# Graph-attention kernel: the queue and the place from which twelve adjacency loads are issued

## The chip, the cores and the metric

The kernel runs on one core of one Trainium2 chip. The metric is the device time of one execution in microseconds, the median over several executions.

## What is computed

The layer is a graph attention with 16 heads over 2048 nodes, followed by a residual and a layer norm. The adjacency matrix is 2048 x 2048 in f32, and x is 2048 x 512.

```
seq = (x @ W_seq).reshape(N, H, DH)              # N 2048, H 16, DH 32
scores = leaky_relu(score1[:, :, None] + score2[:, None, :], 0.2)
scores = scores + (1.0 - adj)[None] * -65500.0
hidden = einsum('hij,jhd->ihd', softmax(scores), seq).reshape(N, 512)
out = layernorm(x + elu(hidden @ W_out + b_out))
```

## The kernel before

The 2048 nodes are 16 tiles of 128 rows. All tiles, loops and loads are counted from 0 here, so the first adjacency tile is 0 and the last is 15.

**First stage (to about 51 us).** For each tile t of x, SyncE loads it (`load_x`, L298, 256 KB), TensorE turns it (`turn_x`, L387), ScalarE copies the turned tile out of PSUM (`copy_x`, L581), and TensorE multiplies it with the first half of the weights (`project`, L400). TensorE's order is: turn tile t+1, project tile t, turn tile t+2, project tile t+1. Turning tile t needs its load; projecting it needs its copy. VectorE copies the results (`copy_first`, L787 and L788).

**The adjacency.** Beside this the adjacency matrix goes through four steps, tile by tile:
1. a load of 1 MB of f32 into one of `STAGE` = 4 buffers (`load_adj`, L303). Tile t uses the buffer t % 4, so from tile 4 on it waits until the cast of tile t - 4 is done (semaphore `adj_cast`);
2. a cast to int8 by ScalarE (`cast_adj`, L592), which also sums the row;
3. a correction of empty rows by VectorE (`fix_adj`, L779 and L782);
4. a DMA transpose from `tring` to `adj8`, issued by SyncE (`turn_adj`, L316).

ScalarE's order is written out by hand. While x is projected, iteration t copies tile t+1 and then casts the tiles that the table `CAST_AT` (L57) gives for it: tile 0 at t = 1, tile 1 at t = 2, tile 2 at t = 4, tile 3 at 6, tile 4 at 7, tile 5 at 9, tile 6 at 11, tile 7 at 13 and tile 8 at 14. Copies of the first head's row (`copy_row0`, L601) lie between them. Casts 9 to 15 are in the second stage (L656 to L682), between copies of the second projection (`copy_second`, L597), two exponentials (L663, L665), and the high halves of the values (`split_high`, L631), for each of which VectorE makes the input (`values`, L860) and then the low half (`split_low`, L866).

SyncE's order is written out too. It issues x tiles 0 to 7 and adjacency tiles 0 to 3 alternately (L310 to L326), and then the loop over t below: the load of adjacency tile t + 4, two x tiles, the transpose of tile t. Each instruction of SyncE waits for those ahead of it, so the load of tile t + 5 comes behind the transpose of tile t. An x load from tile 6 on waits until TensorE has turned the tile six before.

```
            for t in range(NT):
                if t + STAGE < NT:
                    load_adj(t + STAGE)
                for n in range(8 + 2 * t, min(10 + 2 * t, NT)):
                    load_x(n)
                turn_adj(t)
```

**Second stage (about 51 to 93 us).** TensorE makes the second half of the projection (`project_second`, L416) and the first products of head 0 (L475); ScalarE and VectorE make the values of the first heads and the masks of head 0 (ScalarE: L614; VectorE: L811, joined with the adjacency in L816). Masks go into the slots of `tring` that the transposes have read.

**Third stage (from about 93 us).** For each head, TensorE multiplies masks with values (L475), with the sums over the plain adjacency behind (L489). The output projection and the layer norm follow (L556, L568 and further).

Of the kernel before, what the change touches and what calls it, by code (L numbers as in the profile page):

```python
# [16 lines left out]
NT = N // P  # L17
# [25 lines left out]
XS, STAGE, TURNED = 6, 4, 8  # L43
# [50 lines left out]
def gat_kernel(nc, x, adj, W_seq, a1, a2, W_out, b_out, out):  # L94
    with ExitStack() as ctx:
# [3 lines left out]
        def sem(name):  # L99
            return ctx.enter_context(nc.semaphore(name))  # L100
# [25 lines left out]
        stage = flat[:, 4 * HV:4 * HV + 2 * STAGE * N].bitcast(F32).rearrange("p (r n) -> p r n", r=STAGE)  # L126
# [56 lines left out]
        adj_loaded = [sem(f"adj_loaded{r}") for r in range(STAGE)]  # L183
# [4 lines left out]
        adj_cast, noedge_set, adj_fixed = (sem(s) for s in ("adj_cast", "noedge_set", "adj_fixed"))  # L188
# [31 lines left out]
        adj_n = adj.rearrange("(q p s) n -> q s p n", p=P, s=2)  # L220

        def x_t(t):
            return x_n[t // 2, t % 2]
# [12 lines left out]
        def wait_turned(eng, it):  # L236

            eng.wait_ge(adj_turned[it % TURNED], 16 * (it // TURNED + 1))
# [34 lines left out]
        def row(h):  # L273

            return abc[:, (h + 1) % 2, :] if h > 0 else row0
# [8 lines left out]
        def load_a(eng, r, a):  # L284

            eng.dma_start(a_row[:, r, :].rearrange("p (q d) -> p q d", d=DH),
                          a.rearrange("(o q d) -> o q d", o=1, q=1).to_broadcast([1, P // DH, DH])).then_inc(a12_loaded, 16)

        def load_w(eng, k):
            eng.dma_start(Wx[:, k, :, 0:half], W_seq[k * P:(k + 1) * P, :].rearrange("p (s c) -> p s c", s=2)).then_inc(w_loaded[k], 16)  # L290


        @block.sync
        def _(sp):
            def load_x(t):
                if t >= XS:
                    sp.wait_ge(x_turned, t - XS + 1)
                sp.dma_start(xs[:, t % XS, :], x_t(t)).then_inc(x_loaded[t % XS], 16)  # L298

            def load_adj(t):  # L300
                if t >= STAGE:
                    sp.wait_ge(adj_cast, t - STAGE + 1)
                sp.dma_start(stage[:, t % STAGE, :], adj_n[t // 2, t % 2]).then_inc(adj_loaded[t % STAGE], 16)  # L303

            load_a(sp, 0, a1)
            load_x(0)
            for k in range(0, KT, 2):
                load_w(sp, k)
            for t in range(1, XS - 2):
                load_x(t)  # L310
            def turn_adj(it):

                sp.wait_ge(adj_fixed, it + 1)
                if it >= TURNED:
                    wait_turned(sp, it - TURNED)
                sp.dma_start(adj8[:].bitcast(F16)[:, :, it * P:(it + 1) * P],  # L316
                             tring[:, it, :].bitcast(F16), transpose=True).then_inc(adj_turned[it % TURNED], 16)

            load_adj(0)
            load_x(4)  # L320
            load_adj(1)
            load_x(5)
            load_adj(2)
            load_x(6)
            load_adj(3)
            load_x(7)  # L326
            for t in range(NT):
                if t + STAGE < NT:
                    load_adj(t + STAGE)
                for n in range(8 + 2 * t, min(10 + 2 * t, NT)):  # L330
                    load_x(n)
                turn_adj(t)

            sp.wait_ge(a_copied, 1)
            for t in range(4):

                sp.dma_start(scratch.rearrange("h (g t n) -> t h g n", g=4, t=4)[t],
                             aT[2 * H * t:2 * H * t + H, :].rearrange("p (g n) -> p g n", g=4)).then_inc(a_stored[t], 16)
            for t in range(4):
                sp.wait_ge(a_stored[t], 16)  # L340
            for h in range(1, H):
                if h == 2:
                    sp.wait_ge(seq2_made, NT)
                if h >= 2:
                    sp.wait_ge(t_ready, NT * (h - 1))
                if h == 5:

                    sp.wait_ge(mx2_ready, 1)
                    sp.dma_start(scratch2.rearrange("o (p h) -> (o p) h", p=P), mx2).then_inc(mx2_stored, 16)
                    sp.wait_ge(mx2_stored, 16)  # L350
                    sp.dma_start(peaks, scratch2[0:1, :].partition_broadcast(P)).then_inc(peaks_loaded, 16)
                sp.dma_start(row(h), scratch[h:h + 1, :].partition_broadcast(P)).then_inc(abc_loaded[h % 2], 16)

            sp.wait_ge(t_ready, NT * (H - 1))
            sp.dma_start(Wo_sb, W_out.rearrange("(k p) n -> p k n", p=P)).then_inc(wo_loaded, 16)
            sp.wait_ge(t_free, NT * (H - 2))
            sp.dma_start(bout, b_out.rearrange("(o d) -> o d", o=1).partition_broadcast(P)).then_inc(bout_loaded, 16)
            for i in range(NT + 2):
                r = i % 2
                if i < NT:  # L360
                    if i >= 2:
                        sp.wait_ge(y_ready, i - 1)
                    sp.dma_start(xr[:, r, :], x_t(i)).then_inc(xr_loaded[r], 16)
                if i >= 2:
                    if i <= NT:
                        sp.wait_ge(out_ready, i - 1)
                    else:
                        sp.wait_ge(out_last, 1)
                    sp.dma_start(out_n[(i - 2) // 2, i % 2], ot[:, r, :]).then_inc(stored[r], 16)
            for q in range(2):  # L370
                sp.wait_ge(stored[q], 16 * NT // 2)
# [202 lines left out]
        def _(act):  # L574
            load_a(act, 1, a2)
            for k in range(1, KT, 2):
                load_w(act, k)
# [9 lines left out]
            def cast_adj(it):  # L587
                r = it % 4
                act.wait_ge(adj_loaded[it % STAGE], 16 * (it // STAGE + 1))
                if it >= 4:  # L590
                    act.wait_ge(noedge_set, it - 3)
                act.activation(tring[:, it, :], stage[:, it % STAGE, :], ACT.Copy, scale=EDGE,  # L592
                               accum_out=deg[:, r:r + 1]).then_inc(adj_cast, 1)

            def copy_second(t):
                act.wait_ge(seq2_made, t + 1)
                act.copy(seq[:, t, HALF:H, 0:DH], second_bank(t).rearrange("p (h d) -> p h d", d=DH)).then_inc(seq2_copied, 1)  # L597
# [18 lines left out]
            for t in range(NT):  # L616
                if 0 < t < NT - 1:
                    copy_x(t + 1)
                for it in CAST_AT.get(t, ()):
                    cast_adj(it)  # L620
                if t in (5, 9, 13):
                    copy_row0(t // 4 - 1)
# [31 lines left out]


            cast_adj(9)  # L656
            copy_second(0)
            copy_row0(3)
            cast_adj(10)
            copy_second(1)  # L660
            copy_second(2)
# [74 lines left out]
            for i in range(NT):  # L736
                r, q = i % 2, (i - 1) % 2
                if i >= 2:
                    act.wait_ge(y_ready, i - 1)
                for n, (c, _) in enumerate(column_parts(i, r)):  # L740
                    act.wait_ge(z_ready, i + 1 + n)

                    act.activation(et[:, r, c], zt[:, r, c], ACT.Relu, scale=-1.0).then_inc(zneg_ready, 1)  # L743
                    act.wait_ge(zneg_ready, i + 1 + n)
                    act.activation(et[:, r, c], et[:, r, c], ACT.Exp, scale=-1.0).then_inc(e_ready, 1)
                if i + 2 < NT:
                    turn_hidden(i + 2)
                if i >= 1:
                    act.wait_ge(shift_ready, i)
                    if i >= 3:  # L750
                        act.wait_ge(stored[q], 16 * ((i - 1) // 2))
                    act.activation(ot[:, q, :], yt[:, q, :], ACT.Identity, bias=shift[:, q:q + 1],  # L752
                                   scale=rstd[:, q:q + 1]).then_inc(out_ready, 1)
# [419 lines left out]
```

## Time and profile before

| what | value |
|---|---|
| median of 3 runs | 519.34 us (519.14 to 520.39) |
| profiled execution, its own time | 520.75 us |
| its span | 519.0 us |
| TensorE matmul busy | 501.0 us (97%) |
| VectorE busy | 460.2 us (89%) |
| ScalarE busy | 433.0 us (83%) |
| DMA queue of SyncE (q1) | 51.79 MB, 30.2% of 16 engines' span |
| DMA queue of ScalarE (q10) | 0.52 MB, 0.3% |
| adjacency loads, issue to landing | 16, median 8.4 us |

Busy shares are of the span, from the profiler; 1.75 us of the profiled execution lie outside its span. The granted TensorE clock is at its full level in all of the 40 slices but the last. A DMA has two times in the profile: the issue, which keeps the issuing engine's queue, and the landing, when the data is there and the semaphore rises. Busy shares of the DMA engines are sums of the packets' times, and can be over 1 where packets overlap.

### The profile page before, as it was taken

What the parts mean: (1) busy time and instruction counts of PE and PEld (TensorE: products, weight loads), DVE (VectorE), ACT (ScalarE), POOL (GpSimd) and SP (SyncE); (2) the same over time, 40 slices, a digit from 0 to 9 for tenths busy, and PEclk for the clock granted to TensorE, in tenths of its full rate; (3) what the DMA queues carried; (4) which work ended last, traced back from release to release, by engine and by line L of the source; (5) the groups of instructions that cost most, each with busy time, mean ns of one, the idle gap of its engine ahead of it and who ended that gap; (6) DMA issues with size and microseconds to landing.
All of it is one profiled execution on the core that took longest, in us unless ns stands there. A gap on an engine that the chain in (4) does not pass through costs nothing.

```text
span 519.0 us, 15251 instructions
## 1 busy us (share of the span) xinstructions
PE 501.0 (97%) x6744; PEld 454.4 (88%) x6744; DVE 460.2 (89%) x577; ACT 433.0 (83%) x462; POOL 34.8 (7%) x64
## 2 busy tenths in 40 slices
PE   8999999999999989999999999999999999899993
PEld 7888888999999989999999999999999999644542
DVE  3457679998999999999999999999998879988886
ACT  2776779798999889999999999999995989266664
POOL 3000000000000010000000000000000000035444
PEclk9999999999999999999999999999999999999998
DMA  7999993402020301202021020202202040025443
GB/s 249 414 313 343 342 304 72 164 3 82 3 83 2 124 30 55 83 3 83 3 83 56 30 83 3 83 1 83 80 7 82 3 144 3 1 68 155 125 142 120
DMA packets 30721, 53.28 MB, mean 103 GB/s; under 512 B 18496, under 2 KB 19776, under 8 KB 26688
## 3 DMA queue, kind: packets, MB, share of 16 engines
q1 hardware_dynamic: 30104, 51.79, 30.2%
q8 instruction: 53, 0.87, 0.7%
q10 hardware_dynamic: 552, 0.52, 0.3%
q14 instruction: 12, 0.10, 0.1%
HBM read 43.78 MB, written 4.33 MB: 93 GB/s over the span
## 4 chain that ended last, share of the span: by engine, by line
PE 73%; DVE 13%; ACT 6%; issue 4%; DMA 3%; POOL 0%; ACTq 0%; DVEq 0%; POOLq 0%; SPq 0%
PE sums L475 35%; PE bank L489 18%; PE sums L568 10%; PE sums L400 6%; DVE tring L816 4%; ACT tring L614 3%; DVE tring L811 3%; DMA Vp<-in_adj_dram 1%; PE bank L556 1%; PE sums L387 1%; DVE Vp L866 1%; DMA Vp<-in_L_gnn_W_seq_dram 1%; DVE Vp L792 1%; ACT Vp L631 1%; DVE xp L860 1%
## 5 line engine op out<-in xcount | busy, mean ns | idle before, releaser
L614 ACT ACTIVATE tring<-abc,ab 128x2048 int8<-128x2048 f32 x150 | 292.4, 2023 | 2.7 <-DMA abc<-a_rows 2.7
L475 PE MATMUL sums<-Vp,tring 128*128 128x132 f16 x4096 | 241.6, 221 | 3.6 <-DVE tring L816 1.9
L475 PEld LDWEIGHTS sums<-Vp,tring 128*128 128x128 fp8e4 x4096 | 236.9, 98 | 5.6 <-issue 3.5
L816 DVE TENSOR_TENSOR tring<-adj,tring 128x1024 uint32<-128x1024 uint32 (+1 forms) x134 | 155.9, 1174 | 11.7 <-ACT tring L614 7.5
L489 PE MATMUL bank<-Vp,adj 128*128 128x132 f16 x2048 | 126.1, 221 | 3.3 <-DVE Vp L866 3.3
L489 PEld LDWEIGHTS bank<-Vp,adj 128*128 128x128 fp8e4 x2048 | 122.1, 96 | 3.7 <-DVE Vp L866 3.6
L811 DVE TENSOR_SCALAR tring<-abc,ab 128x2048 int8<-128x2048 f32 x90 | 115.5, 1284 | 0.0
L568 PE MATMUL sums<-abc,Vp 128*128 128x512 f32 (+1 forms) x136 | 57.5, 568 | 0.1
L568 PEld LDWEIGHTS sums<-abc,Vp 128*128 128x128 f32 x136 | 24.7, 190 | 22.7 <-issue 22.0
L652 ACT ACTIVATE low<-sums 128x33 f32<-128x33 f32 (+3 forms) x66 | 20.1, 393 | 22.3 <-PE sums L475 22.3
L592 ACT ACTIVATE tring<-Vp 128x2048 int8<-128x2048 f32 x16 | 30.6, 1914 | 5.9 <-DMA Vp<-in_adj_dram 5.9
L752 ACT ACTIVATE Vp<-Vp 128x512 f32<-128x512 f32 x15 | 12.2, 813 | 16.4 <-POOL Vp L1146 16.4
L866 DVE SCALAR_TENSOR_TENSOR Vp<-Vp,xp 128x528 f16<-128x528 f16 x32 | 21.2, 706 | 3.6 <-ACT Vp L631 3.6
L879 DVE TENSOR_TENSOR cab<-low,sums 128x66 f32<-128x66 f32 (+3 forms) x33 | 21.2, 682 | 1.4 <-ACT low L652 1.4
L637 ACT ACTIVATE acc<-bank 128x132 f32<-128x132 f32 x64 | 18.8, 294 | 2.8 <-PE bank L489 2.7
L631 ACT ACTIVATE Vp<-xp 128x528 f16<-128x528 f32 x32 | 19.6, 678 | 1.7 <-DVE xp L860 1.7
L860 DVE TENSOR_TENSOR xp<-acc,Es 128x1056 f32<-128x1056 f32 x16 | 20.1, 1254 | 0.1
L811 DVE TENSOR_SCALAR tring<-cab,ab 128x2048 int8<-128x2048 f32 (+2 forms) x16 | 14.7, 950 | 3.1 <-DMA adj<-tring 2.5
L743 ACT ACTIVATE Vp<-Vp 128x512 f32<-128x512 f32 (+1 forms) x17 | 10.2, 602 | 8.3 <-DVE Vp L1042 8.2
L1042 DVE TENSOR_TENSOR Vp<-sums,Vp 128x512 f32<-128x512 f32 (+1 forms) x17 | 11.2, 658 | 6.6 <-PE sums L568 6.6
L400 PE MATMUL sums<-Vp,acc 128*128 128x288 f32 x64 | 17.0, 406 | 0.0
L787 DVE COPY ab<-sums 128x32 f32<-128x32 f32 x16 | 3.0, 189 | 13.7 <-PE sums L400 13.7
(116 smaller groups left out, 370.3 us busy)
## 6 DMA issues: line engine op xcount, KB each, us to landing
Vp<-in_adj_dram SPq DMA_DIRECT2D x16, 1024.0 KB, 8.4
abc<-a_rows SPq DMA_DIRECT2D x15, 1024.0 KB, 4.8
abc<-in_x_dram SPq DMA_DIRECT2D x16, 256.0 KB, 7.3
Vp<-in_x_dram SPq DMA_DIRECT2D x16, 256.0 KB, 3.0
out_dram<-Vp SPq DMA_DIRECT2D x16, 256.0 KB, 2.2
abc<-in_L_gnn_W_out_dram SPq DMA_DIRECT2D x1, 1024.0 KB, 5.3
Vp<-in_L_gnn_W_seq_dram ACTq DMA_DIRECT2D x2, 256.0 KB, 5.4
Vp<-in_L_gnn_W_seq_dram SPq DMA_DIRECT2D x2, 256.0 KB, 6.1
```

What stands on the lines that cost most here:

```text
L400: mm = pe.matmul(first_bank(t), xT_part(t, k), Wx[:, k, 0, :], start=(k == BY_VECTOR[0]), stop=(k == BY_VECTOR[1]))
L475: mm = pe.matmul(bank[b][:, c * 2 * VW:(c + 1) * 2 * VW], slot(jt)[:, it * P:(it + 1) * P].bitcast(F8), Vp[:, h, jt, :, :], start=(jt == 0 ...
L489: mm = pe.matmul(bank[6 + s % 2][:, 0:GRP * HW], edge_bytes[:, jt // 2, it * P:(it + 1) * P, jt % 2].bitcast(F8), Vp[:, GRP * g:GRP * (g + ...
L568: mm = pe.matmul(into, hT[:, q, k * P:(k + 1) * P], Wo_sb[:, k, c], start=(k == 0), stop=(k == KT - 1))
L592: act.activation(tring[:, it, :], stage[:, it % STAGE, :], ACT.Copy, scale=EDGE, accum_out=deg[:, r:r + 1]).then_inc(adj_cast, 1)
L614: return act.activation(slot(jt)[:, columns], row(h)[:, columns], ACT.Sign, bias=ab[:, jt, H + h:H + h + 1], scale=-1.0)
L631: high = act.activation(Vp[:, k, :, 0, s * HW:(s + 1) * HW], xp[:, :, s, :], ACT.Copy, scale=1.0 / LO[s])
L811: return dve.tensor_scalar(slot(jt)[:, columns], row(h)[:, columns], ab[:, jt, H + h:H + h + 1], -1.0, ALU.is_gt, ALU.mult)
L816: return dve.tensor_tensor(words, edges, words, ALU.bitwise_and)
L860: dve.tensor_tensor(xp[:], seq[:, :, k, :].unsqueeze(2).to_broadcast([P, NT, 2, HW]), Es[:, :, :, k:k + 1].to_broadcast([P, NT, 2, HW]), A ...
L866: low = dve.scalar_tensor_tensor(out=Vp[:, k, :, 1, s * HW:(s + 1) * HW], in0=Vp[:, k, :, 0, s * HW:(s + 1) * HW], scalar=-LO[s], in1=xp[: ...
L879: return dve.tensor_tensor(into, lo, high, ALU.add)
```

## The change

`load_adj` becomes a helper that takes the issuing engine. SyncE keeps the loads of adjacency tiles 0 to 3. The loads of tiles 4 to 15 leave SyncE's loop, and ScalarE issues each one directly behind the cast of the tile four before; ScalarE waits for that cast (`adj_cast`) ahead of the issue. Buffers, semaphores, casts and transposes are unchanged.

```diff
+        def load_adj(eng, t):
+            if t >= STAGE:
+                eng.wait_ge(adj_cast, t - STAGE + 1)
+            eng.dma_start(stage[:, t % STAGE, :], adj_n[t // 2, t % 2]).then_inc(adj_loaded[t % STAGE], 16)
...
-            def load_adj(t):
-                if t >= STAGE:
-                    sp.wait_ge(adj_cast, t - STAGE + 1)
-                sp.dma_start(stage[:, t % STAGE, :], adj_n[t // 2, t % 2]).then_inc(adj_loaded[t % STAGE], 16)
...
-            load_adj(0)
+            load_adj(sp, 0)
...
             for t in range(NT):
-                if t + STAGE < NT:
-                    load_adj(t + STAGE)
                 for n in range(8 + 2 * t, min(10 + 2 * t, NT)):
                     load_x(n)
                 turn_adj(t)
...
                 act.activation(tring[:, it, :], stage[:, it % STAGE, :], ACT.Copy, scale=EDGE,
                                accum_out=deg[:, r:r + 1]).then_inc(adj_cast, 1)
+                if it + STAGE < NT:
+                    load_adj(act, it + STAGE)
```

## Rows read from the trace of the kernel before

**Rows 1.** The chain that ended last, in order of time (start us, us, what).
```profile
56.62 7.50 DMA Vp<-in_adj_dram
...
67.34 1.34 DVE Vp L866 x2
...
93.11 9.38 PE sums L475 x160
```

**Rows 2.** Busy time by stretches: from:to and length, engines (instructions), PEclk, DMA share, GB/s.
```profile
10.00:25.00 15.00, 15.00 (x91) 12.55 (x90) 8.30 (x20) 9.28 (x14) 1.07 (x1) 1.00 1.02 419
...
10.00:51.40 41.40, 41.40 (x224) 33.89 (x223) 24.22 (x63) 27.47 (x39) 1.07 (x1) 1.00 1.07 361
...
68.00:93.00 25.00, 23.17 (x224) 21.01 (x222) 24.55 (x34) 21.64 (x29) 0.00 (x0) 1.00 0.61 179
```

**Rows 3.** Waits: ScalarE from 51 to 68 us, then all from 0 to 70 us (total, times, longest).
```profile
ACT tring L592 <- DMA Vp<-in_adj_dram: 4.6, 4, 2.8
...
DVE Vp L866 <- ACT Vp L631: 3.6, 1, 3.6
```

**Rows 4.** SyncE in order of time (start us, us, instruction).
```profile
17.81 0.33 SPq L303 DMA_DIRECT2D Vp<-in_adj_dram  x1
...
19.14 6.82 SPq L316 DMA_TRANSPOSE adj<-tring  x1
26.01 0.57 SPq L303 DMA_DIRECT2D Vp<-in_adj_dram  x1
```

**Rows 5.** Line 298, stretches 1.6 to 1.8, 8.5 to 13 and 13 to 13.6 us.
```profile
L298 SPq DMA_DIRECT2D abc<-in_x_dram x1: 479/479/479, 1.6 to 1.6; - x1
...
DMA to landing us min/median/max: 2.7/2.7/2.7
...
L298 SPq DMA_DIRECT2D abc<-in_x_dram x1: 666/666/666, 8.8 to 8.8; - x1
...
DMA to landing us min/median/max: 13.5/13.5/13.5
...
L298 SPq DMA_DIRECT2D abc<-in_x_dram x1: 328/328/328, 13.4 to 13.4; - x1
...
DMA to landing us min/median/max: 12.1/12.1/12.1
```

**Rows 6.** Line 303, stretch 8.1 to 9 us.
```profile
L303 SPq DMA_DIRECT2D Vp<-in_adj_dram x1: 592/592/592, 8.2 to 8.2; - x1
...
DMA to landing us min/median/max: 13.6/13.6/13.6
```

**Rows 7.** TensorE in order of time, 17 to 35 us.
```profile
22.23 2.11 PE L400 MATMUL sums<-Vp,acc 128*128 128x288 f32 x8
...
24.61 0.60 PE L387 MATMUL sums<-Vp,abc 128*128 128x128 f32 x4
...
26.99 0.60 PE L387 MATMUL sums<-Vp,abc 128*128 128x128 f32 x4
```

**Rows 8.** ScalarE in order of time.
```profile
2.06 1.28 ACTq L290 DMA_DIRECT2D Vp<-in_L_gnn_W_seq_dram  x2
...
17.59 0.19 ACT L592 ACTIVATION_READ_ACCUMULATOR tring<-Vp 128x1 f32 x1
...
18.16 1.91 ACT L592 ACTIVATE tring<-Vp 128x2048 int8<-128x2048 f32 x1
...
22.92 1.91 ACT L592 ACTIVATE tring<-Vp 128x2048 int8<-128x2048 f32 x1
...
48.49 1.93 ACT L592 ACTIVATE tring<-Vp 128x2048 int8<-128x2048 f32 x1
...
66.05 1.19 ACT L631 ACTIVATE Vp<-xp 128x528 f16<-128x528 f32 x2
```

**Rows 9.** DMA queues, 4.5 to 6.5 us (packets, MB, share of 16 engines).
```profile
q1 hardware_dynamic: 252, 0.25, 40.8%
q10 hardware_dynamic: 265, 0.25, 36.6%
```

More of the change, by code:

```diff
@@ L317, in turn_adj @@
                              tring[:, it, :].bitcast(F16), transpose=True).then_inc(adj_turned[it % TURNED], 16)
-            load_adj(0)
+            load_adj(sp, 0)
             load_x(4)
-            load_adj(1)
+            load_adj(sp, 1)
             load_x(5)
-            load_adj(2)
+            load_adj(sp, 2)
             load_x(6)
-            load_adj(3)
+            load_adj(sp, 3)
             load_x(7)
             for t in range(NT):
-                if t + STAGE < NT:
-                    load_adj(t + STAGE)
                 for n in range(8 + 2 * t, min(10 + 2 * t, NT)):
```

## The prediction

> **What bounds the kernel now.** I read the chain that ended last first, because it names the stretch in which the change acts. It runs through TensorE up to 51 us, then through a load of an adjacency tile (56.62 to 64.1 us), the low half of head 0's values on VectorE at 67.34, and back into TensorE at 93.11 [rows 1]. The busy times say why. From 10 to 51.4 us TensorE is busy for all of 41.40 us: any hole there moves the end. From 68 to 93 us VectorE is busy for 24.55 of 25 us, so what counts between 51 and 67 us is when its run from 67.34 can begin [rows 2]. That run waits 3.6 us for ScalarE's `split_high` [rows 3], which stands behind casts 9 to 12, and these four wait 4.6 us for their loads [rows 3]. This wait is what the change can win.
>
> The third view is the DMA share: 1.02 from 10 to 25 us at 419 GB/s, and 1.07 up to 51.4 us [rows 2]. The DMA engines have no idle time in the first stage. Whatever is brought forward there pushes something else back.
>
> **What SyncE's queue does.** Tile 4's load is issued at 17.81. Two x loads and transpose 0 follow, whose issue holds SyncE for 6.82 us from 19.14, and only then, at 26.01, comes the load of tile 5 [rows 4], though cast 1 ran from 18.16 to 20.07 [rows 8]. So the loads of 5 and later are some 5 us late against their casts, as the diff has it. They are also behind all x loads issued before them, in one queue.
>
> **The change part by part.**
>
> *Twelve issues leave SyncE.* One takes 0.33 to 0.59 us in the rows read [rows 4, 6], so about 7 us go. SyncE is not on the chain. The x loads and transposes behind them are issued earlier; I cost that at nothing, the cover being the full DMA queue.
>
> *Twelve issues come to ScalarE.* Its own two weight loads took 1.28 us, 0.64 each [rows 8]. Before each, ScalarE now waits until the cast has ended with its row sum, at 17.78 for cast 0 [rows 8]; I put 0.1 us on that wait. I take 0.64 + 0.1 = 0.75 us each. In the first stage, the copy of an x tile is what queues behind the issue, and TensorE wants it 2.4 us after the turn (22.23 to 24.61 is one period [rows 7]); the copy takes 0.6 us. So 1.8 us of lateness is covered, and one issue fits. Two casts in consecutive iterations make 1.5 us: it fits too. If the issue took 1 us or more, 0.2 us or more per such pair would show. Cost here: 0.
>
> *Between 48.49 and 66.05* ScalarE goes from cast 8 to `split_high` of head 0 [rows 8]. Four loads (tiles 12 to 15) are now issued within it, behind casts 8 to 11: 4 x 0.75 = 3.0 us. Cast 8 itself starts 0.8 us late behind the load issued after cast 7. The waits of casts 9 to 12 for loads vanish, since these are now issued 8 us and more before use: 4.6 us [rows 3]. Sum: 3.0 + 0.8 - 4.6 = -0.8 us; VectorE's run would begin 0.8 us earlier, and all behind it with it. The bounds: with issues of 0.33 us, 4 x 0.43 + 0.4 - 4.6 = -2.5 us; with 1.3 us each, twice the rows', 5.6 + 1.4 - 4.6 = +2.4 us.
>
> *The order on the DMA engines.* The load of tile 4 used to stand behind x tiles 6 and 7 in SyncE's queue. It now has a queue of its own. How two queues share the engines is seen where the weights are loaded from both: between 4.5 and 6.5 us q1 moved 252 packets and q10 265 [rows 9]: packet by packet, one each. An adjacency packet is a row of 8 KB, an x packet one of 2 KB. At 419 GB/s a tile of 1 MB takes 2.5 us and an x tile 0.6 us [rows 2]. Both have 128 packets, so beside an adjacency load an x tile takes 0.6 + 2.5 = 3.1 us, and another adjacency tile 5.0 us.
>
> [...]
>
> Now the walk. Before, tile 2 landed at 8.2 + 13.6 = 21.8 [rows 6], x6 at 8.8 + 13.5 = 22.3 and x7 at 13.4 + 12.1 = 25.5 [rows 5]. TensorE wanted x6 at 24.61 and x7 at 26.99 [rows 7]: 2.3 and 1.5 us to spare. An x load alone lands after 2.7 us [rows 5], of which 0.6 is data, so an issue acts on landings some 2.1 us later.
> 1. Tile 4, issued by ScalarE behind cast 0 at 17.85, acts from 19.9. By then tile 2 has 1.9 us to go, 6 packets of 8 per engine. Alternating, it takes 3.8 us: tile 2 lands at 23.7.
> 2. Cast 1, 0.8 us later than before, ends at 20.9, so tile 5 is issued at 21.0 and is there. x6 alternates with it: 3.1 us, landing at 26.8. TensorE is 2.2 us late.
> 3. Cast 2 runs at 23.8 instead of 22.92 [rows 8], so tile 6 is issued at 25.8 and acts from 27.9. Tile 3 has 8 packets: 2 beside the end of tile 5 (1.25 us, 28.0), 6 beside tile 6 (3.75 us, 31.8).
> 4. x7 has two packets of tile 6 beside it: 1.2 us, landing at 33.0. TensorE wanted it at 26.99: 6.0 us late in all (x6's 2.2 us are within it).
>
> Then it ends, because copy 7 stands ahead of cast 3 on ScalarE, and so no load of tile 7 is issued until x7 is there. x8 and x9 have the engines nearly to themselves, and later x loads find ScalarE's loads 2.4 us and more apart. The bounds: if only tile 4 gets ahead of x7, 25.5 + 2.5 = 28.0, a stall of 1.0 us; if tiles 4 and 5 do, 3.5 us. I take 6.0, since the weights' packets alternated one to one. Below 1.0 us it needs a queue of ScalarE that yields.
>
> The 6.0 us are not won back. ScalarE's copies and casts 3 to 8 follow TensorE, and from cast 8 to `split_high` ScalarE would run without waits, so `split_high` comes 6.0 - 0.8 = 5.2 us later; VectorE's full run and head 0 with it. TensorE has 1.8 us of idle time between 68 and 93 us [rows 2], which does not help, since VectorE is the one that is full.
>
> **Sum.** 6.0 - 0.8 = +5.2 us: the profiled execution of 520.75 (span 519.0) would take 526.0. It stands 1.4 us above the median of the runs shown; I put the difference on the median: 519.3 + 5.2 = 524.5 us. A measurement of this kernel can tell about 0.3%, 1.6 us, from no change.
>
> **Rivals.**
>
> *The issue on ScalarE waits for SyncE's transposes.* Tile 5's load would be issued at 21.0, in the middle of transpose 0's 6.82 us, which end at 25.96 [rows 4]. If one issue excludes the other, ScalarE stands 4.9 us, the copy of x4 ends at 27.2 instead of before 22.23 [rows 7], and TensorE loses about 4.9 us. Tiles 5 and 6 then come too late to hurt x7. The issues behind casts 9 to 11 would meet transposes too, which between 51 and 67 us hold SyncE most of the time. Of their lengths only transpose 0's is in my rows; as an estimate I take a fifth to a quarter of its 6.8 us for each of the three, 4 us. Sum: 4.9 + 4 - 0.8 = +8.1, 527.4 us. Against it: in the rows, ScalarE's two issues beside SyncE's took only 0.64 us each [rows 8], but no transpose was there. [...] No row of before shows it or excludes it. Chance 0.23.
>
> *A milder jam.* Tile 4, or tiles 4 and 5, get ahead of x7: stalls of 1.0 to 3.5 us, in all +0.2 to +2.7, so 519.5 to 522.0 us. Chance 0.15, a fifth of it within 0.3%.
>
> *Not slower: x keeps its place.* If ScalarE's queue delays x6 by less than 2.3 us and x7 by less than 1.5 us, TensorE sees nothing and only ScalarE's sum counts: -0.8, 518.5 us. The deciding point is whether x7 still lands before 26.99. Against it stand the DMA share of 1.02 and one packet each in the weights. Chance 0.15.
>
> *Faster by more:* the same with issues of 0.33 us, -2.5, so 516.8 us. Chance 0.05.
>
> **How the numbers follow.** The forecast has 0.42: 524.5 us. Slower by over 0.3% (above 520.9) holds forecast, first rival and four fifths of the milder jam: 0.42 + 0.23 + 0.12 = 0.77. Within 0.3%: 0.15 + 0.03 = 0.18. Faster: 0.05. The range leaves out the fastest case and, above, a lock that costs more than I put on it: from 518.5, the case without a jam, to 528.5, the first rival with 1 us more. The forecast's own range, with stalls of 4 to 7 us, is 522.5 to 525.5.
>
> **What would show it.** In the profile after: TensorE, busy throughout from 10 to 51 us before, has holes in front of L387 between 24 and 34 us, which wait for a DMA of x. The landing of x7 grows from 12.1 to some 19 us. Tile 5's load is issued near 21 us from ScalarE's queue, with 0.6 us; if it takes some 5 us instead, the first rival is right, and the hole lies before L400 near 22 us and waits for ScalarE's copy. The waits of casts 9 to 13 for loads are gone. VectorE's first L866 starts near 72.6 instead of 67.34, and the heads' steady part starts as much later. If TensorE has no hole before 51 us, the forecast is wrong; if it has one and the end does not move, my claim that VectorE's run carries it through is.

## The result and the profile after

The changed kernel takes 554.81 us (median of 4 runs, 550.29 to 567.88); the kernel before took 519.52 us beside it (519.14 to 520.39). The ratio is 1.0639, with a 95% interval of 1.0603 to 1.0674: slower by 35.3 us in the medians. The ratio leaves out the longest of the changed kernel's runs, which stands over 1.5% above the fastest; the median of the other three is 551.84 us, 32.3 us above the kernel before. I had forecast 524.5 us and a range up to 528.5. The direction was right, the size was not: the loss is over six times the 5.2 us that I had worked out, and outside the range.

The profiled execution is the longest of the four, 567.88 us with a span of 566.1 us. A second profile of the same kernel, further down, has a span of 542.5 us and the same pattern, milder. First the page of the longest: busy time, then the span in 40 slices of 14 us.

```profile
PE 513.0 (91%) x6744; PEld 462.8 (82%) x6744; DVE 460.4 (81%) x577; ACT 434.0 (77%) x462; POOL 34.8 (6%) x64
...
PE   9955537698999999899999999999999999999994
...
DVE  3431118199999999989999999999999878988886
ACT  2632344467999998889999999999998699646764
...
PEclk9986787989999999899999999999999999999998
DMA  8999899984220103112021020120220103004443
GB/s 287 416 113 246 190 40 264 161 102 123 76 77 1 77 2 114 34 45 76 2 76 76 2 78 19 59 76 2 76 77 2 76 6 129 1 20 145 135 130 130
```

The busy times of VectorE and ScalarE are those of before within 1 us (460.2 and 433.0 us). What has grown is mostly idle time, in slices 3 to 10; TensorE's busy time has grown too, from 501.0 to 513.0 us, where its granted clock is lower. The DMA share stays at 8 and 9 tenths up to slice 9, where before it was down to 3 tenths in slice 7, but in slices 3 to 6 the GB/s are 113, 246, 190 and 40, where the kernel before moved 304 to 343. The same in stretches (from:to and length, the engines, PEclk, DMA share, GB/s), first the changed kernel:

```profile
10.00:25.00 15.00, 15.00 (x91) 12.52 (x89) 7.08 (x19) 9.00 (x14) 0.00 (x0) 1.00 1.02 417
25.00:50.00 25.00, 12.97 (x54) 9.23 (x53) 5.79 (x16) 6.89 (x10) 0.00 (x0) 0.81 1.09 187
50.00:76.00 26.00, 19.41 (x80) 15.00 (x78) 3.76 (x10) 12.45 (x17) 0.00 (x0) 0.79 1.20 182
76.00:105.00 29.00, 16.98 (x76) 14.07 (x75) 14.34 (x38) 12.91 (x22) 0.41 (x1) 0.82 1.13 179
```

The kernel before:

```profile
25.00:50.00 25.00, 25.00 (x129) 20.20 (x128) 14.52 (x39) 17.68 (x24) 0.00 (x0) 1.00 1.11 327
50.00:76.00 26.00, 25.26 (x143) 21.45 (x142) 19.48 (x41) 18.70 (x31) 0.40 (x1) 1.00 1.11 338
```

Up to 25 us nothing has changed: 417 GB/s at a share of 1.02, before 419 at 1.02 [rows 2]. From 25 us on the share stays above 1, and the rate falls to 179 to 187 GB/s up to 105 us. Before, it was 327 and 338 GB/s at 1.11 from 25 to 76 us. The DMA engines are reported as full as before, and move little more than half as much. The granted clock of TensorE is at a mean of 0.79 to 0.82 here, a mix of stretches at full level (1.00 from 31.0 to 36.9 us) and at half of it (0.50 from 44 to 54 us); from 25 to 50 us it was busy for only 12.97 us.

The chain that ended last names what is waited for, and [rows 1] is its counterpart (start us, us, what):

```profile
27.40 21.15 DMA abc<-in_x_dram
...
54.75 28.32 DMA adj<-tring
...
94.53 16.88 DMA adj<-tring
...
138.82 9.38 PE sums L473 x160
```

Before, there was one adjacency load of 7.50 us in it. Now there is an x load of 21 us and two transposes of 28 and 17 us. The piece of 160 products, with which the steady part of the heads begins, starts at 138.82 instead of 93.11 us, 45.7 us later, and the span is 47.1 us longer (566.1 against 519.0): little was lost behind it. In the second profile the piece of 160 products begins at 116.65, 23.5 us later, and the span is 23.5 us longer.

The next rows are ScalarE in order of time (start us, us, instruction), to compare with [rows 8]; line 292 is `load_adj` here:

```profile
17.52 0.36 ACTq L292 DMA_DIRECT2D Vp<-in_adj_dram  x1
...
20.44 0.33 ACTq L292 DMA_DIRECT2D Vp<-in_adj_dram  x1
```

SyncE in order of time, to compare with [rows 4]:

```profile
18.45 8.90 SPq L316 DMA_TRANSPOSE adj<-tring  x1
...
30.01 16.16 SPq L316 DMA_TRANSPOSE adj<-tring  x1
...
54.75 76.46 SPq L316 DMA_TRANSPOSE adj<-tring  x13
```

ScalarE's issues take 0.33 to 0.36 us, also the one at 20.44, in the middle of transpose 0's 8.90 us. SyncE is held for 16.16 us by transpose 1, and the last 13 transposes keep it for 76.46 us. The view of line 316, all transposes (count: ns min/median/max, first and last start), and then the landings of the same 16 in the kernel before:

```profile
L316 SPq DMA_TRANSPOSE adj<-tring x16: 1232/4670/16157, 18.4 to 130.0; - x16
...
DMA to landing us min/median/max: 3.1/17.4/28.3
```

```profile
DMA to landing us min/median/max: 3.1/7.8/11.0
```

The view of line 303, `load_x` here, once around 13.1 us (x7) and once around 27.4 us (x10), to compare with [rows 5]:

```profile
L303 SPq DMA_DIRECT2D abc<-in_x_dram x1: 328/328/328, 13.1 to 13.1; - x1
...
DMA to landing us min/median/max: 13.7/13.7/13.7
...
L303 SPq DMA_DIRECT2D abc<-in_x_dram x1: 1792/1792/1792, 27.4 to 27.4; - x1
...
DMA to landing us min/median/max: 21.1/21.1/21.1
```

Before, the 16 transposes landed after 3.1 to 11.0 us, 7.8 in the median. Now the median is 17.4 us and the longest takes 28.3; in the second profile the median is 9.1 us and the longest 26.3, so there it is a few transposes that are very slow. x7 took 1.6 us more than before [rows 5] and landed at 26.8, but x10 took 21.1 us. TensorE in order of time shows what that did, with [rows 7] for before (in brackets the idle time ahead and what ended it):

```profile
26.89 0.66 PE L385 MATMUL sums<-Vp,abc 128*128 128x128 f32 x4
...
29.89 0.66 PE L385 MATMUL sums<-Vp,abc 128*128 128x128 f32 x4 [0.40 <-DMA abc<-in_x_dram]
...
35.54 0.66 PE L385 MATMUL sums<-Vp,abc 128*128 128x128 f32 x4 [3.05 <-DMA abc<-in_x_dram]
36.03 3.15 PE L398 MATMUL sums<-Vp,low 128*128 128x288 f32 x8
...
48.59 1.11 PE L385 MATMUL sums<-Vp,abc 128*128 128x128 f32 x4 [8.55 <-DMA abc<-in_x_dram]
```

The hole that I had forecast at x7 is not there. The holes begin with x8 (0.40 us), and the large one, 8.55 us, is x10's. The row at 36.03 also shows the lower clock: eight products take 3.15 us at a granted clock of 0.64 in the mean, and 2.11 us at the full one [rows 7].

### The profile page after: what moved, and what is told of

Read it like the earlier page. It is cut to its first block, busy times and chain, and to the rows that moved or that the text cites. A ratio compares the mean times of both kernels' runs of the same rounds, so it can differ in the third digit from the quotient of the medians.

```text
span 566.1 us, 15251 instructions
## 1 busy us (share of the span) xinstructions
PE 513.0 (91%) x6744; PEld 462.8 (82%) x6744; DVE 460.4 (81%) x577; ACT 434.0 (77%) x462; POOL 34.8 (6%) x64
## 2 busy tenths in 40 slices
DMA packets 30721, 53.28 MB, mean 94 GB/s; under 512 B 18496, under 2 KB 19776, under 8 KB 26688
## 4 chain that ended last, share of the span: by engine, by line
PE 66%; DVE 13%; DMA 12%; ACT 5%; issue 4%; POOL 0%; DVEq 0%; POOLq 0%; ACTq 0%
PE sums L473 32%; PE bank L487 17%; PE sums L566 9%; DMA adj<-tring 8%; DMA abc<-in_x_dram 4%; DVE tring L816 4%; DVE tring L811 3%; ACT tring L614 3%; PE sums L398 3%; PE bank L554 1%; DVE Vp L866 1%; PE sums L385 1%; PE sums L377 1%; DVE Vp L792 1%; PE sums L414 1%
## 5 line engine op out<-in xcount | busy, mean ns | idle before, releaser
L487 PE MATMUL bank<-Vp,adj 128*128 128x132 f16 x2048 | 127.7, 222 | 3.4 <-DVE Vp L866 3.4
L487 PEld LDWEIGHTS bank<-Vp,adj 128*128 128x128 fp8e4 x2048 | 123.8, 97 | 3.8 <-DVE Vp L866 3.8
L652 ACT ACTIVATE low<-sums 128x33 f32<-128x33 f32 (+3 forms) x66 | 20.1, 393 | 23.9 <-PE sums L473 23.9
L385 PE MATMUL sums<-Vp,abc 128*128 128x128 f32 x64 | 11.6, 312 | 18.6 <-DMA abc<-in_x_dram 18.6
L385 PEld LDWEIGHTS sums<-Vp,abc 128*128 128x128 f32 x64 | 8.9, 160 | 22.3 <-DMA abc<-in_x_dram 20.9
L414 PE MATMUL sums<-Vp,acc 128*128 128x256 f32 x64 | 16.1, 409 | 12.0 <-DVE acc L788 12.0
L752 ACT ACTIVATE Vp<-Vp 128x512 f32<-128x512 f32 x15 | 12.2, 813 | 16.4 <-POOL Vp L1146 16.4
L414 PEld LDWEIGHTS sums<-Vp,acc 128*128 128x128 f32 x64 | 12.9, 208 | 14.4 <-DVE acc L788 12.5
L866 DVE SCALAR_TENSOR_TENSOR Vp<-Vp,xp 128x528 f16<-128x528 f16 x32 | 21.2, 706 | 0.0
## 6 DMA issues: line engine op xcount, KB each, us to landing
Vp<-in_adj_dram ACTq DMA_DIRECT2D x12, 1024.0 KB, 18.6
```

The lines of the kernel that those rows point to most:

```text
L385: mm = pe.transpose(bank[r][:, k * P:(k + 1) * P], xs[:, t % XS, k * P:(k + 1) * P], idf)
L414: mm = pe.matmul(second_bank(t), xT_part(t, k), Wx[:, k, 1, 0:half], start=(k == 0), stop=(k == KT - 1))
L487: mm = pe.matmul(bank[6 + s % 2][:, 0:GRP * HW], edge_bytes[:, jt // 2, it * P:(it + 1) * P, jt % 2].bitcast(F8), Vp[:, GRP * g:GRP * (g + ...
L652: copied = act.activation(into, made, ACT.Copy, scale=1.0 / LO[s])
L866: low = dve.scalar_tensor_tensor(out=Vp[:, k, :, 1, s * HW:(s + 1) * HW], in0=Vp[:, k, :, 0, s * HW:(s + 1) * HW], scalar=-LO[s], in1=xp[: ...
```

## The experiments

There were eleven kernels to run: ten new ones, and the changed one again. The kernel before ran beside them on the same chip; its medians were 520.14 us for the first four, 519.64 for the next four and 519.99 for the last three.

| kernel | median us | against before, us | ratio and 95% interval |
|---|---|---|---|
| plain copies, loads as before | 521.56 | +1.4 | 1.0022 (1.0003 to 1.0041) |
| plain copies, loads as changed | 522.78 | +2.6 | 1.0052 (1.0035 to 1.0070) |
| tiles 10 to 15 on ScalarE | 533.93 | +13.8 | 1.0271 (1.0209 to 1.0332) |
| early loads, SyncE alone | 522.18 | +2.0 | 1.0031 (1.0005 to 1.0056) |
| one load on ScalarE | 521.43 | +1.8 | 1.0033 (1.0015 to 1.0052) |
| x tiles 8 to 15 on ScalarE | 523.13 | +3.5 | 1.0065 (1.0043 to 1.0086) |
| packets of 2 KB | 539.73 | +20.1 | 1.0406 (1.0358 to 1.0454) |
| early loads from tile 9 on | 519.22 | -0.4 | 0.9991 (0.9973 to 1.0010) |
| every other tile on ScalarE | 529.68 | +9.7 | 1.0198 (1.0150 to 1.0246) |
| strict turns for tiles 10 to 15 | 552.79 | +32.8 | 1.0626 (1.0602 to 1.0649) |
| the changed kernel again | 554.18 | +34.2 | 1.0654 (1.0580 to 1.0728) |

**Is it the transposes?** Two kernels have plain copies of the same rows in place of the transposes, one with the order of before and one with the change. They leave the adjacency out of the result:

```diff
-                             tring[:, it, :].bitcast(F16), transpose=True)
+                             tring[:, it, :].bitcast(F16).rearrange("p (q d) -> p q d", d=P))
...
-                act.activation(tring[:, it, :], stage[...], ACT.Copy, scale=EDGE,
+                act.activation(tring[:, it, :], stage[...], ACT.Copy, scale=0.0,
```

> The kernel before, with each of the 16 DMA transposes replaced by a plain copy of the same bytes in the same 1024 rows of 256 bytes, from the same queue at the same place, and with the cast's scale set to 0, so that every pair of nodes counts as an edge and the order of the adjacency no longer matters (the adjacency is left out of the result). It is the base for the next kernel. Every theory: near the kernel before, 516 to 522 us.

> The changed kernel with the same replacement. Theory 1 (a transpose in SyncE's queue and a load in ScalarE's queue, in flight together, hold each other up many times over): without transposes the loss shrinks from 35 us to what the order of the packets costs, 0 to 8 us over the plain base. Theory 2 (packets of two queues simply alternate, and small packets lose against 8 KB ones whatever they are): the copies have the same packets, so the loss stays, 25 us or more over the plain base. Theory 3 (the waits and issues on ScalarE): also stays.

The change costs 1.2 us here (522.78 against 521.56), not 35 us. The packets are the same in size and nearly in number (30465 against 30721 in the whole execution), and come from the same queues at the same places; only the transposing is gone. Theory 2, in which packets of two queues just alternate, and theory 3, the waits and issues on ScalarE, both fall as causes of the large loss. The view of line 316 of the kernel with the order of before, and then of the one with the change:

```profile
L316 SPq DMA_DIRECT2D adj<-tring x16: 594/606/796, 19.0 to 83.4; - x16
...
DMA to landing us min/median/max: 2.9/8.5/10.7
```

```profile
L316 SPq DMA_DIRECT2D adj<-tring x16: 593/606/4269, 18.3 to 86.2; - x16
...
DMA to landing us min/median/max: 2.9/9.4/15.8
```

The copies land after 9.4 instead of 8.5 us in the median, where the transposes of the changed kernel take 17.4. TensorE of the second one in order of time, and then its stretch from 10 to 51.4 us (columns as in the stretches above):

```profile
28.21 0.66 PE L385 MATMUL sums<-Vp,abc 128*128 128x128 f32 x4 [1.45 <-DMA abc<-in_x_dram]
...
31.37 0.66 PE L385 MATMUL sums<-Vp,abc 128*128 128x128 f32 x4 [0.56 <-DMA abc<-in_x_dram]
...
42.48 0.66 PE L385 MATMUL sums<-Vp,abc 128*128 128x128 f32 x4 [0.94 <-DMA abc<-in_x_dram]
```

```profile
10.00:51.40 41.40, 38.45 (x207) 30.74 (x207) 19.69 (x50) 24.97 (x36) 1.08 (x1) 1.00 1.06 386
```

The effect of my forecast exists in small: x7 comes 1.45 us late, x8 0.56, a later tile 0.94, and from 10 to 51.4 us TensorE is busy for 38.45 of 41.40 us. That is 3.0 us of holes, where I had put 6.0 on x7 alone.

**Are the x loads needed for it?** Tiles 4 to 9 go back to SyncE, so that ScalarE's loads come after nearly all of x:

```diff
-                if it + STAGE < NT:
+                if 10 <= it + STAGE < NT:
                     load_adj(act, it + STAGE)
...
             for t in range(NT):
+                if t + STAGE < 10:
+                    load_adj(sp, t + STAGE)
```

> The changed kernel with only tiles 10 to 15 loaded from ScalarE's queue; tiles 4 to 9 are back in SyncE's loop. By then all x tiles are loaded or nearly so. Theory 1 (transposes and loads of two queues): transposes from about the seventh on land after 15 us and more instead of 8, and the kernel stays 8 to 20 us slower than before. Theory 2 in my prediction's form (x loads starved in the first stage): no x load is left to be starved, so 518.5 to 520 us.

It is 13.8 us slower, with no x load in flight beside ScalarE's loads and TensorE busy for 40.75 of 41.40 us up to 51.4. The loss needs no starved x tile. The view of line 316, all transposes and then the one issued at 46.6 us. The profiled execution is the longest of five, 551.45 us, so the sizes here are those of a bad run:

```profile
L316 SPq DMA_TRANSPOSE adj<-tring x16: 1232/2450/15899, 25.0 to 114.7; - x16
...
who waited for it (us, times):
  DVE tring L818: 27.9, 1
...
DMA to landing us min/median/max: 3.0/7.0/34.8
...
L316 SPq DMA_TRANSPOSE adj<-tring x1: 1503/1503/1503, 46.6 to 46.6; - x1
...
DMA to landing us min/median/max: 27.7/27.7/27.7
```

The transpose of tile 4, issued at 42.0, still landed after 8.5 us. That of tile 5, issued at 46.6, is the first beside ScalarE's queue, whose first load is issued at 48.16; it took 27.7 us, and a later one 34.8. VectorE waits 27.9 us for one of them.

**Is it the early loads, from whatever queue?** Here SyncE issues everything, with each load and its x tiles ahead of the transpose that used to stand before it:

```diff
-            for t in range(NT):
+            for t in range(NT + 1):
...
-                turn_adj(t)
+                if t > 0:
+                    turn_adj(t - 1)
```

> The kernel before with SyncE alone issuing, but the load of tile t + 5 and its two x tiles ahead of the transpose of tile t, so the loads come as early as their buffers allow and never from a second queue. Theory 1 (two queues): no transpose takes much over 8 to 11 us, the waits of casts 9 to 13 (5.9 us) go, and the time is within 1.5 us of the kernel before, on either side. Theory 4 (loads that come early are what starves the x tiles and the transposes, from whatever queue): slower by 10 us or more.

The time is 2.0 us above the kernel before, and its transposes land after 3.0 to 9.6 us, 7.5 in the median. Early loads from one queue do no great harm; theory 4 falls. It was not within the 1.5 us that I had allowed. Transpose 3 is issued at 39.4 instead of 37.4 us, but VectorE's masks wait only 0.9 us for a transpose here, less than the 2.5 us of before, so this does not explain the 2.0 us; what does stays open.

**What does one overlap cost?** Only tile 12's load comes from ScalarE (`if it + STAGE == 12`, and the others in SyncE's loop).

> The changed kernel with a single load, tile 12's, issued from ScalarE; the other eleven are back in SyncE's loop. Theory 1 (an overlap of a transpose and a load of another queue costs by itself): the transposes beside it land after 15 us and more, later ones recover, and the kernel is 1 to 6 us slower than before. Theory 2 (only packets that alternate): one load moves nothing, within 0.5 us of before.

1.8 us slower, inside the expected 1 to 6 us, but the transposes beside it did not take 15 us: all 16 land after 3.0 to 9.3 us. So a single overlap is mild for the transposes, and my picture of it was too dark. Nor can the 1.8 us be put down to the overlap: two kernels in which SyncE issues every load, the plain copies in the old order and the early loads, came out 1.4 and 2.0 us above the kernel before.

**Do six loads cost six times as much, or does it matter that they follow each other?** The six odd tiles from 5 to 15 come from ScalarE (`if it + STAGE in (5, 7, 9, 11, 13, 15)`).

> The changed kernel with the six odd tiles 5 to 15 loaded from ScalarE's queue and the six even ones from SyncE's. As many loads on ScalarE as in the kernel with tiles 10 to 15 (which was 14 us slower than before), but none directly behind another in that queue, and three of them while x tiles are loaded. Theory P (each load that meets a transpose costs its 2 to 3 us, as one_load's 1.8 us and the 14 us of six say): 10 to 18 us slower than before. Theory Q (the damage needs a queue of ScalarE that stays filled beside the transposes; a single load passes in 8 turns): 0 to 6 us slower, and no transpose over 12 us.

The loss is 9.7 us, between the two ranges, and far above that of one load. Six loads in a row cost 13.8 us, but the two intervals overlap (1.0150 to 1.0246 and 1.0209 to 1.0332), so whether the gaps help at all stays open. The longest transpose lands after 13.7 us here; the 34.8 us of the loads in a row come from an execution of 551.45 us and cannot be held against it.

**Does the size of the load's packets matter?** Each of ScalarE's loads is cut into four of 512 columns:

```diff
-            eng.dma_start(stage[:, t % STAGE, :], adj_n[t // 2, t % 2]).then_inc(adj_loaded[t % STAGE], 16)
+            for c in range(4 if t >= STAGE else 1):
+                w = slice(c * N // 4, (c + 1) * N // 4) if t >= STAGE else slice(0, N)
+                eng.dma_start(stage[:, t % STAGE, w], adj_n[t // 2, t % 2][:, w]).then_inc(adj_loaded[t % STAGE], 16)
```

> The changed kernel with each of ScalarE's loads cut into four of 512 columns, so that its packets are 2 KB (0.08 us) and not 8 KB (0.31 us); ScalarE issues 48 loads, about 1 us more per tile. Theory 1a (a transpose's packets go in rows of 16, one per engine, and each row waits for a load packet in between): 64 rows wait 0.08 instead of 0.31 us, about 5 us per transpose instead of 20, and the loss over the kernel before shrinks from 35 us to 10 to 20 us. Theory 1c (each change between the queues has a fixed price): four times as many changes, the loss grows beyond 45 us.

20.1 us instead of 35, just past the edge of what theory 1a allows, although ScalarE has 48 issues and four times as many packets stand against the transposes. A fixed price for each change between the queues (theory 1c) would have made it worse, and falls. The length of the other queue's packets has a part in it, but the transposes still land after up to 20.5 us.

**Does a queue of small plain packets do it too?** In the kernel before, x tiles 8 to 15 come from ScalarE, and all adjacency loads stay with SyncE:

```diff
                     copy_x(t + 1)
+                    if 8 <= t + 7 < NT:
+                        act.dma_start(xs[:, (t + 7) % XS, :], x_t(t + 7)).then_inc(x_loaded[(t + 7) % XS], 16)
```

> The kernel before, but x tiles 8 to 15 come from ScalarE's queue, each behind the copy that frees its buffer; all adjacency loads stay with the transposes in SyncE's queue. A second queue beside transposes, with packets of 2 KB instead of 8 KB. Theory 1a (any packet of another queue stops a row of transpose packets, for its own length): transposes 0 to 4 slow down, by 128 packets of 0.08 us per x tile at most, and the total is 0 to 8 us slower. Theory 1b (only large loads do it): transposes land after 7 to 9 us as before, total within 1.5 us. Either way no stretch of 20 us for one transpose.

3.5 us slower; the first four transposes land after 12.2, 13.7, 10.5 and 9.1 us, where in the kernel before they took 11.0, 7.9, 7.8 and 7.4. So x loads slow them as well, and theory 1b, that only large loads do it, falls. How much of the 3.5 us comes from this is not shown, since a kernel with one queue was already 2.0 us above the kernel before.

**And if the two queues never overlap?** ScalarE's load of tiles 10 to 15 waits until the transpose before has landed, and the transpose until that load has landed:

```diff
+                    wait_turned(act, it - 1)
                     load_adj(act, it + STAGE)
...
                 sp.wait_ge(adj_fixed, it + 1)
+                if 10 <= it + STAGE < NT:
+                    sp.wait_ge(adj_loaded[it % STAGE], 16 * (it // STAGE + 2))
```

> The changed kernel with tiles 10 to 15 from ScalarE's queue, and strict turns: each of these loads is issued only when the transpose before has landed, and each transpose only when the load before has landed. Two queues, no overlap. Theory 1 (the overlap in flight is the cause): transposes from the sixth on land after 3 to 4 us instead of 14 to 35, loads after 5 us instead of 26. Each tile then takes some 9 us in series instead of 4, so the time is no better than the 14 us of the kernel it is made from, 10 to 25 us over before. Theory 2 (two queues cost whether or not they overlap): transposes stay over 6 us.

The view of line 318 around 66 us, one transpose behind such a load:

```profile
L318 SPq DMA_TRANSPOSE adj<-tring x1: 1232/1232/1232, 66.2 to 66.2; - x1
...
DMA to landing us min/median/max: 3.0/3.0/3.0
```

And ScalarE's loads among the DMA issues (count, KB each, median us from issue to landing):

```profile
Vp<-in_adj_dram ACTq DMA_DIRECT2D x6, 1024.0 KB, 5.1
```

The transfers are quick: this transpose lands after 3.0 us and ScalarE's loads after 5.1 us, where in the profile of the overlapping version, its longest run, the same six loads took 26.1 us in the median. So it is the overlap in flight, and not the use of two queues. The total is no gain, as expected, and with 32.8 us worse than the 10 to 25 us that I had put on it. ScalarE itself now waits for the transposes (by its waits, 16.0 us before the copies at L602 and 11.4 us before one at L583), which I had counted only as transfer time.

**Can the wait for the loads be won from one queue?** SyncE alone, with the loads one transpose earlier from tile 9 on, and the first transposes left in place:

```diff
-                if t + STAGE < NT:
+                if t + STAGE < NT and t < 5:
                     load_adj(t + STAGE)
...
+                if t >= 4 and t + STAGE + 1 < NT:
+                    load_adj(t + STAGE + 1)
                 turn_adj(t)
```

> The kernel before, SyncE alone issuing, with the loads of tiles 9 to 15 one transpose earlier (tile t + 5's load ahead of transpose t, from t = 4) and transposes 0 to 3 left where they were. If the waits of casts 9 to 13 are worth what my prediction put on them and transposes stay at 7 to 9 us: 0.5 to 2.5 us faster than before. If the DMA engines' full load takes it back: within 0.5 us.

-0.4 us, with an interval of 0.9973 to 1.0010: no difference. The four waits of casts 9 to 12 fell from 4.6 to 3.2 us only. Nothing that I tried beats the kernel before.

**Once more.**

> The changed kernel once more, for its spread and a second trace. Every theory: 550 to 568 us; transposes land after 14 to 28 us again.

The changed kernel gives 554.18 us (544.29 to 566.07), slightly wider than expected, and in the profiled execution, the shortest of the four, the transposes still land after up to 26.3 us and ScalarE's loads after 12.7 us in the median. Its times scatter over 22 us, where those of the kernel before scatter over 2: how badly the transfers get in each other's way differs from run to run.

**What the DMA engines do during an overlap.** The clearest rows are the queues of the changed kernel from 56 to 62 us, beside the plain version from 34 to 40 us (packets, MB, share of 16 engines; q10 is ScalarE's queue, q1 SyncE's). First the changed kernel:

```profile
q10 hardware_dynamic: 47, 0.36, 92.4%
q1 hardware_dynamic: 237, 0.08, 19.3%
```

The plain version:

```profile
q10 hardware_dynamic: 223, 1.70, 72.5%
q1 hardware_dynamic: 1079, 0.61, 35.2%
```

In the plain version 223 of ScalarE's packets take 72.5% of 16 engines for 6 us: 0.725 x 16 x 6 / 223 = 0.31 us each, which is also what 8 KB take at 419 GB/s over 16 engines. In the changed kernel 47 packets take 92.4%: 0.924 x 16 x 6 / 47 = 1.9 us each. This mean mixes two kinds, as q10's rows of the first and the second 2 us show:

```profile
q10 hardware_dynamic: 20, 0.16, 252.4%
...
q10 hardware_dynamic: 13, 0.10, 11.8%
```

A window counts the whole time of the packets that start in it. The 20 that start from 56 to 58 us take 4.0 us each in the mean, twice the length of the window, so many reach far beyond it. The 13 that start from 58 to 60 us take 0.29 us each. The packet records of the trace say it one by one: 15 of the load packets that start between 55.8 and 57.6 us last 2.1 to 7.4 us, and seven of these end together at 63.54 to 63.57 us, while other load packets pass at the usual 0.3 us. So most of the busy share reported here is load packets that last many times their usual 0.31 us. Of SyncE's 237 packets in these 6 us, 133 start in the first 2 us. In the version with strict turns, where a transpose is alone, it passes all its 1056 packets within the 3.0 us of its landing.

The packets of a transpose can stand as well. The first row is q1 from 76 to 82 us of the changed kernel, with hardly anything but transposes in it; the second is a transpose alone, from 66.2 to 69.3 us of the version with strict turns:

```profile
q1 hardware_dynamic: 238, 0.06, 91.2%
```

```profile
q1 hardware_dynamic: 1056, 0.26, 44.1%
```

That is 0.912 x 16 x 6 / 238 = 0.37 us for each packet, against 0.441 x 16 x 3.1 / 1056 = 0.02 us alone.

The packet records show how they stand. From 77.53 us on the packets of the transpose start in groups of 15 to 17, some 0.33 us apart, each with one load packet beside it. The rows are those of 77.53 to 77.85, 77.86 to 78.18 and 78.19 to 78.50 us:

```profile
q1 hardware_dynamic: 17, 0.00, 124.7%
q10 hardware_dynamic: 1, 0.01, 6.3%
...
q1 hardware_dynamic: 15, 0.00, 139.1%
q10 hardware_dynamic: 1, 0.01, 6.0%
...
q1 hardware_dynamic: 16, 0.00, 150.4%
q10 hardware_dynamic: 1, 0.01, 6.4%
```

Of the first 17 packets, 13 take 0.34 us and end at 77.88 to 77.91 us, as the load packet beside them does at 77.88. Three take 0.65 us and end at 78.19 to 78.21, as the next load packet does at 78.20, and one takes 0.02 us. Of all 238, 29 take 0.02 us, 150 take 0.32 to 0.34 and 59 take 0.63 to 0.65. So in this stretch most packets of the transpose stand for the time of one or two load packets. Why it does is not shown: the traces do not say which engine a packet was on. Why a run in a bad pattern leaves it again also stays open.

## Why the prediction was right and wrong

- **What bounds the kernel** held. The stretch up to 93 us carries every loss straight to the end: 45.7 of 47.1 us in one profile and 23.5 of 23.5 in the other.
- **Twelve issues leave SyncE, "I cost that at nothing, the cover being the full DMA queue".** This is the step that failed. I priced the issue of the transposes and x loads, and not their transfer beside a second queue. The transposes were among the DMAs that the change moved the loads past, and I had no row of before that showed a transpose beside ScalarE's queue; I should have bounded it from both sides. Measured: landings of up to 28.3 us instead of 11.0, with a median of 17.4 instead of 7.8 us (up to 26.3 and 9.1 in the second profile). With plain copies in their place the change costs 1.2 us, so some 34 of the 35 us come from here, the time that TensorE loses at its lower clock in the stretches of waiting among them. So the right direction is mostly luck: what I had worked out is at most a small part of what made the kernel slower.
- **Packet by packet** was applied too widely. It holds between plain transfers: beside the copies, ScalarE's packets kept their 0.31 us. Between a load and a transpose it does not. The rows that I took it from had packets of about one size in both queues [rows 9], and none of a transpose.
- **Twelve issues come to ScalarE** were half as dear as I took them: 0.33 instead of 0.64 us, and all but hidden. The 4.6 us of waits for the loads did go; only 0.5 us stand before the casts, ahead of the wait for ScalarE's own cast.
- **The walk** put x7 at 33.0 us; it landed at 26.8 (28.2 with plain copies). Why the tiles already in SyncE's queue kept more of their lead stays open. With plain copies the hole before x7 was 1.45 us, where I had 6.0, and the other 1.5 us of the 3.0 came at x8 and later, which I had taken to have the engines nearly to themselves. So even the forecast's own mechanism was at least twice too large; the 1.2 us that it left lie within my rival of a milder jam.
- **The sum's last step**, that a stall is not won back, can be judged in the plain version: 3.0 us of holes less 0.8 us gives 2.2 us; the medians differ by 1.2 us and the two spans by 2.9.
- **The first rival**, the issue that waits for the transposes, is refuted: ScalarE's issue takes 0.33 us in the middle of transpose 0's 8.90 us. That one issue excludes the other was an assumption, which no row of before had shown.
- **What would show it**: the holes of TensorE came, but later and larger, before x8 to x10 and not x7. VectorE's first L866 began at 113.05 us and not at 72.6.

## What to carry to other kernels

Keep DMA transposes and large plain transfers that overlap them in one queue, even if the queue looks like a bottleneck: in this kernel every version with transposes and more than one adjacency load in a second queue was slower, by 9.7 to 35 us, and none with all of them in one queue by more than 2.0 us. When a transfer is moved to another queue, ask of every kind of transfer left behind what it costs beside a second queue, and if no row shows that kind beside one, put a wide bound on it. A high DMA share with few GB/s is the sign to look for: here 1.09 at 187 GB/s from 25 to 50 us, against 1.11 at 327 before.

## What I had not expected of the hardware

- A 1 MB load from ScalarE's queue beside transposes from SyncE's landed after 12.7 us in the median in the shortest profiled execution of the changed kernel (18.6 in the longest), and transposes after up to 26.3 us (28.3). In strict turns the two take 5.1 and 3.0 us.
- The loss grows with what overlaps: 9.7 and 13.8 us for six loads, 35 for twelve. The 1.8 us of one load and the 3.5 of eight x tiles are near the 1.4 and 2.0 us of versions with one queue.
- While a transpose and loads of another queue are in flight, some load packets, which otherwise take 0.31 us, stand for 2.1 to 7.4 us in the stretch looked at, and transpose packets take 0.37 us in the mean of another instead of 0.02.
- Cutting the loads into packets of 2 KB brought the loss from 35 to 20.1 us.
- An issue on ScalarE takes 0.33 us even while SyncE's is held by a transpose for 8.90 us.
